# Two-layer decoder on one core: bias row on TensorE, folded scale and paired rstd in the quantized cross attention

## The reference, cut to what matters

```
q = (x @ Wq + bq).reshape(1, B * N, H, hd)
scale = 1.0 / np.sqrt(hd)                       # 1/4, with hd = 16
q = _fq_sym(q * scale, axis=-1)                 # s = max(max|q| / 127, 1e-8); round(q / s), clipped to +-127, times s
attn = softmax(einsum('bhqd,bhkd->bhqk', q, k)) # 512 keys, 16 heads
attn = _fq_unsigned(attn, axis=-1)              # s = max / 255
out = einsum('bhqk,bhkd->bhqd', attn, v) @ Wp + bp
def _layernorm(x): return (x - mean) / sqrt(var + 1e-5)
```

## Time and profile before

| what | value |
|---|---|
| median of 3 runs | 1400.11 us (1394.38 to 1400.13) |
| the profiled execution, its own time | 1389.28 us |
| its span, first to last instruction | 1387.2 us |
| mean granted TensorE clock | 0.911 of 2.4 GHz |
| stage of `Cross1`, first to last row maximum | 803 to 1130 us |

### The profile page before, as it was taken

How to read it: one execution, slowest core, us unless ns; L and a number is a source line. 1 busy time by engine, 2 the same in 40 slices (tenths; PEclk the granted TensorE clock), 3 DMA queues, 4 the chain that set the end, 5 groups by cost and what they waited for, 6 DMA issues and landing times.

```text
span 1387.2 us, 24942 instructions
## 1 busy us (share of the span) xinstructions
PE 1142.9 (82%) x7640; PEld 812.6 (59%) x7679; DVE 898.7 (65%) x2577; ACT 635.2 (46%) x1430; POOL 603.8 (44%) x938
## 2 busy tenths in 40 slices
PE   4699989983999999657888677877778778999988
PEld 3577767772566666445665445545556555687855
DVE  5576764664333333357976589999998974655657
ACT  3165653331211111214554479888888871433310
POOL 6153543446311111224755435566765553355510
PEclk8799999995999999868998879899888888999999
DMA  5766635013111111163551020000000013454454
GB/s 146 190 202 167 192 95 182 32 39 100 48 50 43 45 45 45 54 182 110 136 144 49 14 114 1 6 28 33 33 23 24 21 44 129 114 161 148 153 180 144
DMA packets 75535, 127.12 MB, mean 92 GB/s; under 512 B 11623, under 2 KB 58791, under 8 KB 71911
## 3 DMA queue, kind: packets, MB, share of 16 engines
q1 hardware_dynamic: 61870, 95.13, 24.8%
q0 software_dynamic: 10272, 28.39, 5.6%
q10 hardware_dynamic: 3264, 2.01, 0.5%
HBM read 76.97 MB, written 48.13 MB: 90 GB/s over the span
## 4 chain that ended last, share of the span: by engine, by line
PE 53%; issue 13%; POOL 13%; DVE 7%; ACT 7%; DMA 5%; ACTq 1%; SPq 1%; another core or an unknown queue 0%; POOLq 0%; DVEq 0%
PE ps L228 16%; PE ps L1151 15%; PE ps L1168 7%; POOL work L1908 4%; POOL xs_scratch L1482 3%; ACT work L1874 3%; PE ps L480 3%; DMA W<-work 2%; PE ps L1160 2%; PE ps L1136 2%; DVE work L597 1%; PE ps L303 1%; PE ps L462 1%; PE ps L493 1%; POOL rstd L272 1%
## 5 line engine op out<-in xcount | busy, mean ns | idle before, releaser
L1151 PE MATMUL ps<-W,work 128*128 x628 | 226.6, 494 | 1.9 <-issue 1.8
L1500 POOL DMA_INDIRECT ys_scratch<-work x118 | 113.2, 959 | 263.0 <-DVE work L1344 114.8
L1874 ACT ACTIVATE work<-ps,work 128x512 f32<-128x512 f32 x256 | 202.1, 798 | 36.5 <-POOL work L1908 34.9
L1812 DVE TENSOR_REDUCE work<-ps 128x1 f32<-128x512 f32 x256 | 171.8, 678 | 17.1 <-PE ps L1719 12.4
L1394 DVE TENSOR_TENSOR work<-work,ps 128x128 f32<-128x128 f32 (+1 forms) x118 | 49.6, 420 | 201.5 <-ACT work L1463 169.7
L597 DVE TENSOR_REDUCE work<-ps 128x2 f32<-128x512 f32 (+1 forms) x192 | 127.2, 684 | 77.6 <-PE ps L462 76.5
L769 POOL TENSOR_SCALAR_AFFINE_SELECT work<-work 128x256 f32<-128x256 f32 (+1 forms) x192 | 92.6, 485 | 154.9 <-ACT work L703 153.9
L1908 POOL TENSOR_SCALAR work<-work 128x1 f32<-128x1 f32 x256 | 102.0, 398 | 115.3 <-DVE work L1812 100.7
L1151 PEld LDWEIGHTS ps<-W,work 128*128 128x128 f32 x628 | 110.8, 191 | 68.5 <-issue 63.4
L703 ACT ACTIVATE work<-ps 128x512 f32<-128x512 f32 x192 | 110.5, 598 | 67.5 <-PE ps L480 66.9
L1719 PE MATMUL ps<-SM,work 128*128 128x512 bf16 x217 | 92.7, 430 | 42.8 <-ACT work L1874 38.5
(11 more groups left out here) (256 smaller groups left out, 2401.5 us busy)
## 6 DMA issues: line engine op xcount, KB each, us to landing
work<-xs_scratch SPq DMA_DIRECT2D x79, 132.0 KB
W<-ys_scratch SPq DMA_DIRECT2D x16, 512.0 KB
q_parts<-work SPq DMA_DIRECT2D x48, 128.0 KB, 1.8
W<-q_parts SPq DMA_DIRECT2D x16, 384.0 KB
W<-in_w_in SPq DMA_DIRECT2D x6, 1024.0 KB, 11.3
work<-xs_scratch SPq DMA_DIRECT2D x39, 130.0 KB
W<-k_parts SPq DMA_DIRECT2D x8, 512.0 KB
W<-q_parts SPq DMA_DIRECT2D x16, 256.0 KB
```

Of the source, the lines that this page charges most:

```text
L1151: mm = q.e.matmul(PS[bks[c]][:, 0:N], self.XT[s % 2][:, k, :], w[:, k, bass.ds(regs[s] + 512 * c if c else regs[s], N)], start=k == 0, sto ...
L1500: q.e.indirect_dma_start(YS[L], bass.IndirectOffsetOnAxis(ap=self.dst[n % self.NY], axis=0), self.YB[n % self.NY], None).then_inc(*landing ...
L1812: q.e.tensor_reduce(self.mm[:, h:h + 1], PS[banks.of["c1_s", t, h]][:, :], AX, ALU.max).then_inc(*up("c1_mx", t, h))
L1874: q.e.activation(self.ee[n // 2 % 3][:, 512 * (h % 2):512 * (h % 2) + 512], PS[banks.of["c1_s", t, h]][:, :], ACT.Exp, bias=self.nb[:, h:h ...
```

## The change

In `Cross1`: the queries' bias is no longer added by DVE. `pe_q` gets one more fp32 product ahead of its two, a row of ones (1 x 128) with the bias row (1 x 256), in the same PSUM accumulation. The factor 1/4 is multiplied into `wq1` and `bq1` once by ACT, beside the self attention before (`kv_scalar`). DVE's step list is therefore shorter, takes its input from PSUM twice, and holds the bank three rounds longer. The row maxima are written negated, so POOL uses `sq` in place of `nsq`, and `nsq` and `s4` are gone. `pe_q` now also waits for the scaled weights and for the row of ones, which DVE writes at the start of the stage. The transposes of `ln4` move from h = 5 to h = 7 and their copy from 6 to 8, and the normalizations of `ln5` move from h = 7 and 8 to 8 and 9.

In all stages: `ve` (variance plus 1e-5) is made for two tiles by one instruction after the second tile's statistics, and the power is taken for two tiles by one instruction of 128 x 2 where there were two of 128 x 1.

```diff
@@ layer norms @@
-            q.wait_ge(q.chain())
-            e.tensor_scalar(ve[:, t:t + 1], mv[:, t, 1:2], 1e-5, None, ALU.add).then_inc(*up("ve", s, t))
-
-        def ln_pow1(q, s, t):
-            q.wait_ge(at("consts", "half"), at("ve", s, t))
-            q.e.tensor_tensor(rstd[:, t:t + 1], ve[:, t:t + 1], half[:, :], ALU.pow).then_inc(*up("rstd", s, t))
+            if t % 2:
+                q.wait_ge(q.chain())
+                e.tensor_scalar(ve[:, t - 1:t + 1], mv[:, t - 1:t + 1, 1], 1e-5, None, ALU.add).then_inc(*up("ve", s, t // 2))
+
+        def ln_pow(q, s, p):
+            q.wait_ge(at("consts", "half"), at("ve", s, p))
+            q.e.tensor_tensor(rstd[:, 2 * p:2 * p + 2], ve[:, 2 * p:2 * p + 2], half, ALU.pow).then_inc(*up("rstd", s, p))
...
@@ kv_scalar @@
+                if c == 1:
+
+                    q.wait_ge(at("w_cr1", "bp"))
+                    q.e.mul(wq1, wq1, 0.25)
+                    q.e.mul(bq1, bq1, 0.25).then_inc(*up("wq_s"))
...
@@ pe_q @@
-                q.wait_ge(at("xnT", 4, t // 2), at("w_cr1", "bp"), *free)
-                pair_mms(q, PS[bk][:, 0:256], [(xnt(t)[k], wq1[:, k, :]) for k in range(2)]).then_inc(*up("c1_q", t))
+                q.wait_ge(at("xnT", 4, t // 2), at("w_cr1", "bp"), at("wq_s"), at("c1_z"), *free)
+                pair_mms(q, PS[bk][:, 0:256], [(self.one, bq1[0:1, :]), *[(xnt(t)[k], wq1[:, k, :]) for k in range(2)]]).then_inc(*up("c1_q", t))
...
@@ tensor @@
-                    if h == 5 and self.ln4(t - 1):
+                    if h == 7 and self.ln4(t - 1):
...
@@ dve_queries @@
-                q.wait_ge(at("c1_q", t), *ends(4), at("c1_Q3", t - 1))
-                e.tensor_tensor(qf, PS[banks.of["c1_q", t]][:, 0:256], bq1, ALU.add).then_inc(*up("c1_qf", t))
-                yield
-                q.wait_ge(at("c1_qf", t), at("kv_Vq"))
-                e.tensor_reduce(am, q3, AX, ALU.max, apply_absolute_value=True).then_inc(*q.step())
-                yield
-                q.wait_ge(q.chain())
-                e.tensor_scalar(s4, am, 1.0 / 127.0, 4e-8, ALU.mult, ALU.max).then_inc(*q.step())
...
-                e.tensor_scalar(self.sq[t % 2], s4, 0.25, None, ALU.mult).then_inc(*q.step())
-                e.tensor_scalar(self.nsq[t % 2], s4, -0.25, None, ALU.mult).then_inc(*up("c1_sq", t))
-                e.reciprocal(rq, s4).then_inc(*q.step())
...
+                ps = heads(PS[banks.of["c1_q", t]][:, 0:256], 16)
+                q.wait_ge(at("c1_q", t), *ends(4))
+                e.tensor_reduce(self.am, ps, AX, ALU.max, apply_absolute_value=True).then_inc(*q.step())
                 yield
                 q.wait_ge(q.chain(), at("c1_exp", t - 2, H - 1))
...
+                e.tensor_scalar(sq, self.am, 1.0 / 127.0, 1e-8, ALU.mult, ALU.max).then_inc(*up("c1_sq", t))
+                yield
+                q.wait_ge(at("c1_sq", t))
+                e.reciprocal(self.rq, sq).then_inc(*q.step())
+                yield
+                q.wait_ge(q.chain(), at("c1_Q3", t - 1))
+                e.tensor_tensor(heads(qf, 16), ps, bc(self.rq, 2, 16), ALU.mult).then_inc(*up("c1_qf", t))
...
@@ dve_max @@
-                q.e.tensor_reduce(self.mm[:, h:h + 1], PS[banks.of["c1_s", t, h]][:, :], AX, ALU.max).then_inc(*up("c1_mx", t, h))
+                q.e.tensor_reduce(self.mm[:, h:h + 1], PS[banks.of["c1_s", t, h]][:, :], AX, ALU.max, negate=True).then_inc(*up("c1_mx", t, h))
...
@@ vector @@
+                e.memset(self.one, 1.0).then_inc(*q.step())
...
@@ gpsimd @@
-                    if h in (12, 13) and self.ln4(t):
-                        ln_pow1(q, 4, 2 * self.ln4(t) + h - 12)
+                    if h == 12 and self.ln4(t):
+                        ln_pow(q, 4, self.ln4(t))
```

More of the change, by code:

```diff
@@ L90 @@
     scalar_tensor_tensor = bn_stats = bn_aggr = memset = max = match_replace = copy = activation = same
-    iota = affine_select = dma_start = indirect_dma_start = then_inc = wait_ge = same
+    mul = iota = affine_select = dma_start = indirect_dma_start = then_inc = wait_ge = same
     def value_load(self, *a, **k):
@@ L163, in decoder @@
         rstd = sb("rstd", [128, T])
-        columns = sb("columns", [128, 2])
-        half, slotc = columns[:, 0:1], columns[:, 1:2]
+        columns = sb("columns", [128, 3])
+        half, slotc = columns[:, 0:2], columns[:, 2:3]
         upb = sb("upb", [128, 128], BF)
@@ L284, in ln_stats @@
                 ln_stat(q, s, t)
-        def ln_pow(q, s, p):
-            for t in (2 * p, 2 * p + 1):
-                ln_pow1(q, s, t)
         def ln_norm(q, s, p, base=()):
@@ L796, in gpsimd @@
                 ln_pow(q, self.ln, 1)
-                q.wait_ge(at("rstd", self.ln, 3), *self.base())
+                q.wait_ge(at("rstd", self.ln, 1), *self.base())
                 self.pool_rows(q, 0)
@@ L819, in gpsimd @@
                             self.pool_keep(q, i, u // 3, u % 3)
[L820 to L824, removed]
+                        if i == -1 and u == 1:
+                            ln_pow(q, self.ln, 2)
+                        if self.norms(i) and u == 7:
+                            ln_pow(q, *self.norms(i))
                         if i >= 1 and u in (4, 5):
@@ L1658, in kv_scalar @@
             for c in range(4):
-                for _ in range(3):
-                    yield
+                yield
[4 more added lines that the diff above has]
+                yield
+                yield
                 q.wait_ge(at("kv_v", c), *kv_base())
@@ L1674, in __init__ @@
                 self.q3T = [wk(512, BF).rearrange("p (g n) -> p g n", g=8) for _ in range(2)]
-                self.sq, self.nsq = [wk(16) for _ in range(2)], [wk(16) for _ in range(2)]
-                self.rq, self.s4, self.mm, self.nb = wk(16), wk(16), wk(16), wk(16)
+                self.sq = [wk(16) for _ in range(2)]
+                self.rq, self.mm, self.nb = wk(16), wk(16), wk(16)
                 self.se, self.rs = [wk(16) for _ in range(2)], wk(16)
+                self.one = wk(128)[0:1, :]
                 self.ee = [wk(1024) for _ in range(3)]
@@ L1857, in vector @@
                         ln_stat(q, 5, 2 * self.ln5(t) + h - 5)
-                    if h in (7, 8) and self.ln5(t) is not None:
-                        ln_norm1(q, 5, 2 * self.ln5(t) + h - 7, ends(4))
+                    if h in (8, 9) and self.ln5(t) is not None:
+                        ln_norm1(q, 5, 2 * self.ln5(t) + h - 8, ends(4))
                     if h == 1 and self.ln5(t - 1) is not None:
@@ L1889, in scalar @@
                         router_copy(q, 1, self.ln5(t - 1))
-                    if h == 6 and self.ln4(t - 1):
+                    if h == 8 and self.ln4(t - 1):
                         ln_copy(q, 4, self.ln4(t - 1))
@@ L1907, in pool_nb @@
                 q.wait_ge(at("c1_mx", t, h), at("c1_sq", t), at("c1_exp", t - 1, h))
-                q.e.tensor_scalar(self.nb[:, h:h + 1], self.mm[:, h:h + 1], self.nsq[t % 2][:, h:h + 1], LN255, ALU.mult, ALU.add).then_inc(
+                q.e.tensor_scalar(self.nb[:, h:h + 1], self.mm[:, h:h + 1], self.sq[t % 2][:, h:h + 1], LN255, ALU.mult, ALU.add).then_inc(
                     *up("c1_nb", t, h))
@@ L1917, in gpsimd @@
                         self.pool_nb(q, *self.unit(i - 1))
-                    if h in (6, 7) and self.ln5(t) is not None:
-                        ln_pow1(q, 5, 2 * self.ln5(t) + h - 6)
+                    if h == 7 and self.ln5(t) is not None:
+                        ln_pow(q, 5, self.ln5(t))
                     if h == 10 and t + 1 < T:
@@ L1946, in vector_program @@
             e = q.e
-            e.memset(half[:, :], -0.5).then_inc(*up("consts", "half"))
+            e.memset(half, -0.5).then_inc(*up("consts", "half"))
             q.wait_ge(at("c", "sq"))
```

11 lines of the change are left out of this document (4 added, 7 removed).

## The result

The change made the kernel slower: 1414.94 us (median of 4 runs, 1412.04 to 1422.57) against 1397.49 us for the kernel before (4 runs, 1394.38 to 1400.13), a ratio of 1.0134, 95% interval 1.0085 to 1.0184. Forecast were 1395.4 us and a range of 1387 to 1404; the time lies outside of it. The profiled execution took 1422.57 us, with a span of 1420.6 and a mean granted clock of 0.903.

A forecast was written before the change was run, and what follows sets the result against it. The prediction took DVE as the pace of most rounds in the second layer's cross attention. Terms of 11.6 us off and 6.9 on made 4.7 off the median 1400.11: 1395.4 us, range 1387 to 1404.

The forecast's parts named there:

- One more product in `pe_q`: Ahead of the scores of h = 2, the added product counts in full in 11 tiles: 5.9 us on.
- The clock at that place: At `pe_q`, the stage's mean clock of 0.87 was taken: half clock 26% of the time, 0.54 us a product.
- DVE's saving: In rounds 3 to about 12, paced by DVE: 7.2 us off for queries and 2.6 for `ve`.
- POOL and ACT pace the rounds: Rival in the stage's rounds: DVE's shorter list only makes it wait; 5.1 us slower, 1405.2 us, chance 0.13.
- the sign that DVE was not the pace: In the stage, DVE's idle time growing by 8 us or more outside of h = 2.
- The pairs: Paired `ve` and powers: in the stage 2.6 and 1.2 us off; elsewhere 0.6 off, 0.7 on at the starts.
- The power: On POOL, a power for two tiles takes 0.70 us; 1.2 us off in six odd tiles with `ln4`.
- `ve`: On DVE in the stage, 0.2 us less for each of 13 pairs: 2.6 us off.
- the queries' shorter list: On DVE in tiles 1 to 15, bias and scaling instructions go: 0.48 us a tile, 7.2 us off.
- the input from PSUM: DVE's reduction and multiplication for the queries now read PSUM: no difference in time.
- the harmless transposes of `ln4`: Moved behind scores of h = 7, PE waits in six even tiles; DVE needs h = 8 only later: nothing.
- where DVE would wait: At the maximum of h = 2, 1.0 us in odd tiles in place of 0.58; none at h = 9.

The follow-up runs named there:

- before_row: The kernel before with only the one-row product added to `pe_q`, its left side zeros: 1409.49 us, ratio 1.0127.
- either kind of fillers: Unread bf16 products added on PE behind the scores of three heads, restarting or keeping sums; kernel before: 0.9942 and 0.9944, changed kernel: 1.0033 and 1.0104.
- second trace: The changed kernel and the kernel before, each run and profiled once more without any change: 1414.31 and 1391.76 us.
- noprod: The changed kernel without the one-row product, the queries' bias left out of the result: 1392.71 us, ratio 1.0032 to the kernel before.
- pairs: The kernel before with only the paired `ve` and powers, `ln5` normalizations one round later: 1393.23 us, ratio 1.0030.
- queries_keep: The kernel before with only the queries' part, its bias as three bf16 parts, plus sum-keeping fillers, single powers: 1382.12 us, ratio 0.9900.
- before_keep: The kernel before with only the fillers that keep the open sums added: 1386.56 us, ratio 0.9944.

## Why the prediction was wrong

**The step that failed** is "One more product in `pe_q`". Its mechanism was right: the product lies ahead of the scores of h = 2, and DVE waits there. Its size was not, 5.9 us for what cost 17.6 alone (`before_row`). The price of the product was wrong, and that is shown: with a bias of 0.11 us in its place the changed kernel went from 1.0134 to 1.0012, and with either kind of fillers from 1.0033 to 0.9917 and from 1.0104 to 0.9925. The clock at the place was also not as taken, which the traces show, but what that cost is not shown apart.

- *The price of one product.* I took it as dear as a full one and put the bounds at "0 and that". It lies above that bound: 0.73 us at full clock against 0.43, and 1.31 against 0.85 at half. Giving the product 128 rows, and changing nothing else in `pe_q`, brought the ratio from 1.0134 to 1.0079, where the intervals overlap, and with fillers from 1.0104 to 0.9997, where they do not (that of the other run with fillers, 1.0033, does overlap with 0.9997). With 0.73 and 1.31 us and the clock of the forecast the term is 11 x (0.74 x 0.73 + 0.26 x 1.31) = 9.7 us.
- *The clock at that place.* I took the stage's mean, half clock in 26% of the time. At h = 1 it was 80% in the changed kernel (66% in its second trace), where it was 24% (33%) before. In tile 11 the clock is down for `pe_q`, the transposes and the scores, which are on the path. What brings it down in one tile and not in another is not shown: ahead of it PE idled 1.09 and 0.38 us, but in tile 11 of before it idled 1.00 and 0.38 and kept the full clock. With 0.8 the term is 11 x (0.2 x 0.73 + 0.8 x 1.31) = 13.1 us, and the two old products and the transposes at that place slow down as well: `pe_q` took 25.4 us more in all (18.7 in the second pair of traces), the new product included.

The Trainium skill ("TensorE: Matmul & The Clock Gate", Part 1) says that idle TensorE falls to 1.2 GHz. The traces have that level, and with fillers at PE's idle places the time at it in the stage of before fell from 85.5 to 47.9 us; the two tiles 11 show that single waits of this size do not decide it. Part 2 of the page, cited beside this term for time by columns alone, is not enough for this shape: at full clock one row of fp32 weights took 304 to 320 ns from record to record, and the record of the next product behind it 320, where 128 rows took 216, all of 256 columns.

**DVE's saving** was right where I looked for it, in rounds 3 to 6, and not for the time of the whole. `noprod` has it without the product, and equals `pairs`: 1.0032 and 1.0030. So the queries' part alone gave nothing at the clock as it was. Why is not shown. Against the kernel before, the passage got longer in `noprod` (`pe_q` 20.0 us against 16.0 with the same instructions, the wait at h = 2 13.6 against 8.7), but in `pairs`, which has the kernel before's queries, it is longer still (22.0 and 17.0). With the clock held up by fillers it gave 0.9900 / 0.9944, 0.44%, 6.1 us (4.4 by the difference of the two medians), with a bias of 0.11 us; 7.2 were priced. The intervals of these two overlap, so the size is loose. The forecast's condition for the rival "POOL and ACT pace the rounds" (more than half of DVE's saving turns into idle time) came true. DVE's idle time in the stage grew by 40.6 us, 30.8 of them at h = 2. The other 9.8 us (8.2 in the second pair) lie just over the 8 that the forecast named as the sign that DVE was not the pace; most of them stand in the rounds next to the passage, behind h = 2 and h = 15. But ACT's wait for POOL fell from 34.2 to 30.3 us, so the mechanism of that rival is not what happened.

**The pairs** had the wrong sign. The power costs what I took. What I left out is that the first tile of a pair now waits for the statistics of the second and for a power of 0.73 us where 0.54 did. In the stage, where I priced only POOL's part and `ve`, DVE waits 0.42 us in four odd tiles. At each start there are two pairs and not one (1.27 us of idle time more at each, against 0.35 forecast). In the first cross attention, for which I took 0.6 us off, the idle time ahead of the normalizations grew by 1.1 to 2.1 us, and in the rest of the self attentions, where I had written "I take nothing", by 1.3. The cost is 0.30% by itself (the interval leaves zero out), and by the medians 0.15% with fillers and 0.25% beside the queries' part (0.9925 / 0.9900), where the intervals overlap.

**Right** were `ve` (2.3 us for 2.6), the queries' shorter list (with fillers, the rounds h = 3 to 14 took 14.76 us a tile in `queries_keep` and 15.25 in `before_keep`, 0.49 off where 0.48 were priced), the input from PSUM, the harmless transposes of `ln4`, and where DVE would wait. The chance of 0.10 for slower was too small because the only way there led through rivals; the term with the widest unknown, a row of ones that no trace had shown, was bounded by a neighbour of another shape, and its clock was taken as given, though with the change it is another.

**Open** stays how the 17 us divide between the product's price and the clock, since each slower passage also changes PE's idle time: the corrected price makes 9.7 us at the clock of the forecast and 13.1 at 80% half clock, both short of it. Also open is why the two filler runs of the changed kernel differ, 1.0033 and 1.0104, with the same work on PE and nearly the same share at half clock (.24 and .25); their intervals exclude each other, and every statement on 'with fillers' for that kernel is as loose as that.

## What to carry to other kernels

Work moved to an engine with room (PE at 77% of the stage) lands at a place, not in a mean: read the wait right behind that place, and the clock of that place. A bias row through the array is cheap as one bf16 product of its three parts (0.11 us) and dear as one fp32 row (0.73). Where PE stands at half clock in the critical passage, a few products that nobody reads can be worth as much as a shorter list elsewhere (0.56% here, and 0.44% for DVE's list behind them); pair small operations only where both results are used late.

## What the runs showed of the hardware

- An fp32 product with one row of weights and 256 columns took 0.73 us, one with 128 rows 0.43, and a bf16 one 0.11 (all at full clock).
- A power of 128 x 2 on POOL took 0.73 us, where 128 x 1 took 0.59 in the mean: the second column is neither free nor the price of another instruction.
- Fillers made the kernel before faster by 0.56% (0.9944 [0.9907, 0.9981]): half-clock time in the stage fell from 85.5 to 47.9 us, and DVE's wait at h = 2 from 8.7 to 5.8, in one trace each.
- A start flag on other columns of a bank changed the sums that were open in it; accumulating into those columns did not. The Trainium skill ("PSUM — Partial Sum Buffer", "The four PSUM rules") says that such a flag clears, over the whole bank, the marks by which later products add to a sum, and the changed outputs agree.
